# Causal attention in four head groups: blocks of two groups taken alternately, rising then falling

## The reference

```
q = einsum('bthc,oc->btho', xh, Wq) * scale
k = einsum('bthc,oc->btho', xh, Wk) * scale
v = einsum('bthc,oc->btho', xh, Wv)
scores = einsum('bihc,bjhc->bhij', q, k)
scores = where(j > i, -inf, scores)
attn = softmax(scores)
y = einsum('bhij,bjhc->bihc', attn, v)
```

## Time and profile before

| what | us |
|---|---|
| median of three runs | 2280.57 |
| lowest and highest | 2272.59, 2297.14 |
| the profiled execution | 2295.76 |
| its span, first to last instruction | 2293.9 |
| TensorE busy in the span | 2093.4 (91%) |
| VectorE busy | 1768.3 (77%) |
| ScalarE busy | 1439.4 (63%) |
| GpSimd busy | 518.1 (23%) |

### The profile page before, as it was taken

One profiled execution on the slowest core, in us unless ns is written; L12 is line 12 of the kernel. 1 busy time (PEld: TensorE's weight loads), 2 busy tenths in 40 slices (PEclk: granted clock), 3 DMA queues, 4 the chain that ended last, 5 costly groups with the idle time before them and its releaser, 6 DMA issues. The chain is left out here.

```text
span 2293.9 us, 43529 instructions
## 1 busy us (share of the span) xinstructions
PE 2093.4 (91%) x17338; PEld 1091.1 (48%) x17338; DVE 1768.3 (77%) x2212; ACT 1439.4 (63%) x2798; POOL 518.1 (23%) x772
## 2 busy tenths in 40 slices
PE   7689999999999999999999999999885959999994
PEld 5233333334444443444444433333365748787883
DVE  6476799999999878899999987776358636666666
ACT  5234577778888877678888888888732323333331
POOL 2000001100110100110111010000163646666661
PEclk9755799999999999999999999999976879999997
DMA  6815011111611111521111011000074323333336
GB/s 232 241 29 65 29 34 39 53 36 34 102 51 34 44 35 39 82 54 34 44 49 60 25 41 37 23 14 12 2 260 186 130 76 110 115 114 113 115 114 243
DMA packets 120813, 180.75 MB, mean 79 GB/s; under 512 B 15793, under 2 KB 80306, under 8 KB 119842
## 3 DMA queue, kind: packets, MB, share of 16 engines
q1 hardware_dynamic: 111904, 154.45, 23.7%
q0 software_dynamic: 6720, 19.01, 2.3%
q10 hardware_dynamic: 1986, 4.51, 0.5%
HBM read 99.92 MB, written 77.60 MB: 77 GB/s over the span
## 5 line engine op out<-in xcount | busy, mean ns | idle before, releaser
L775 DVE TENSOR_REDUCE mx<-S 128x2 f32<-128x1024 f32 (+3 forms) x1152 | 1279.7, 1134 | 206.1 <-PE S L688 131.8
L756 ACT ACTIVATE prob<-ST 128x512 f32<-128x512 f32 (+3 forms) x2304 | 1169.5, 559 | 360.0 <-PE ST L709 315.5
L723 PE MATMUL O<-prob,V 128*17 128x256 f32 (+1 forms) x8704 | 690.6, 391 | 0.3 <-POOL prob L666 0.3
L688 PE MATMUL S<-K,Q 48*128 48x512 f32 (+3 forms) x2304 | 573.9, 496 | 31.4 <-DVE mx L775 20.6
L709 PE MATMUL ST<-Q,K 49*128 49x512 f32 (+3 forms) x2304 | 493.5, 425 | 36.3 <-ACT prob L756 30.8
L688 PEld LDWEIGHTS S<-K,Q 48*128 48x128 f32 x2304 | 225.3, 192 | 472.6 <-issue 297.0
L666 POOL TENSOR_SCALAR_AFFINE_SELECT prob<-prob 128x512 f32<-128x512 f32 x128 | 81.4, 636 | 1217.6 <-ACT prob L756 1217.6
L709 PEld LDWEIGHTS ST<-Q,K 49*128 49x128 f32 x2304 | 225.3, 192 | 137.7 <-ACT prob L756 105.0
L723 PEld LDWEIGHTS O<-prob,V 128*17 128x17 f32 x8704 | 145.6, 96 | 288.9 <-issue 279.9
L1575 ACT ACTIVATE sg<-hg 128x512 f32<-128x512 f32 x92 | 55.2, 600 | 156.9 <-PE hu L1504 152.9
L1683 DVE TENSOR_TENSOR alo<-sg,ahi 128x512 fp32r<-128x512 f32 x92 | 88.1, 958 | 68.1 <-ACT ahi L1579 63.6
(11 more groups left out here) (238 smaller groups left out, 1765.4 us busy)
## 6 DMA issues: line engine op xcount, KB each, us to landing
cwb<-cwt SPq DMA_DIRECT2D x76, 256.0 KB, 4.9
lists<-wbd SPq DMA_DIRECT2D x132, 138.0 KB, 2.2
Q<-qs SPq DMA_DIRECT2D x192, 64.0 KB, 2.4
xs<-lists SPq DMA_DIRECT2D x19, 552.0 KB
K<-ks SPq DMA_DIRECT2D x18, 512.0 KB, 15.6
qs<-hl SPq DMA_DIRECT2D x16, 512.0 KB, 4.5
ks<-hl SPq DMA_DIRECT2D x16, 512.0 KB, 4.4
wraw<-in_wcat SPq DMA_DIRECT2D x54, 128.0 KB, 2.1
```

What stands on the lines that cost most here:

```text
L688: ins = pe.matmul(out[:, ab, 0:w], Q[g, n % QR, p, r * P:(r + 1) * P], K[G % 2][g, p, c * BW:c * BW + w], start=True, stop=not diag)
L723: ins = pe.matmul(O[32 * a:32 * a + VC, c0:c1], V[:, G, k, VC * a:VC * (a + 1)], prob[:, s % NP, a, c0:c1], start=s in FIRST and h == 0, s ...
L756: act.activation(prob[:, s % NP, 2 * p + ab, c0:BW], ST[u % ST_BANKS][:, c0:BW], ACT.Exp).then_inc(s_exp, 1)
L775: dve.tensor_reduce(mx[:, n % 2, a:a + step + 1:step, c], S[slot % S_RING][:, :, 0:w], AX_X, ALU.max).then_inc(s_free, 1)
```

## The change

`block_order` gives the order (0,0), (0,1), (1,0), (0,2), (1,1), (0,3), (1,2), ... (0,7), (1,6), (1,7), and then the mirror image with groups 2 and 3: (2,7), (2,6), (3,7), (2,5), (3,6), ... (2,1), (3,2), (2,0), (3,1), (3,0). Before, group 0 rose, 1 fell, 2 rose and 3 fell. The marks are now those of all blocks, from which the ones below the upper hull are dropped. K of group 1 is loaded in the three pieces like that of group 0, piece 0 at once, piece 1 at steps 0 to 2 and piece 2 at steps 8 to 10, on the semaphores of group 0's pieces; K of group 2 follows when block (0,7) has been read. Lines are 5 to 16 further down behind the places that the diff touches.

```diff
-BLOCKS = [(G, j) for G in range(NG4) for j in (range(NB) if G % 2 == 0 else range(NB - 1, -1, -1))]
+def block_order():
+    up = [(0, 0)] + [x for j in range(1, NB) for x in ((0, j), (1, j - 1))] + [(1, NB - 1)]
+    return up + [(G + 2, j) for G, j in reversed([(1 - G, j) for G, j in up])]
+
+
+BLOCKS = block_order()
...
-    marks = [(FIRST[n] - 3.0, upto[n]) for n in range(len(BLOCKS)) if n <= NB or n >= 3 * NB]
+    marks = []
+    for n in range(len(BLOCKS)):
+        x, y = FIRST[n] - 3.0, upto[n]
+        while len(marks) > 1 and (marks[-1][1] - marks[-2][1]) * (x - marks[-2][0]) <= \
+                (y - marks[-2][1]) * (marks[-1][0] - marks[-2][0]):
+            marks.pop()
+        marks.append((x, y))
...
+    events.extend(("K", (1, i, 0)) for i in range(6))
     scores(0)
...
-        if 0 <= s - 16 < 6:
-            events.append(("K", (1, s - 16, None)))
+        for i, first in ((1, 0), (2, 8)):
+            if 0 <= s - first < 3:
+                events.extend(("K", (1, 2 * (s - first) + h, i)) for h in range(2))
         for G2 in (2, 3):
-            first = LAST[NUMBER[(G2 - 2, 7 if G2 == 2 else 0)]] + 4
+            first = LAST[NUMBER[(G2 - 2, NB - 1)]] + 4
...
                         if G > 1:
-                            need("st", s_st, HG * (TPB * NB * (NB + 1) // 2) * (G - 1))
-                        load_k_part(sp, t, d, G, i // 3, i % 3, 0, T, s_k[G])
+                            need("st", s_st, units_before(NUMBER[(G - 2, NB - 1)]))
+                            load_k_part(sp, t, d, G, i // 3, i % 3, 0, T, s_k[G])
+                        else:
+                            need(f"piece{piece}", s_piece[piece], 16 * 6)
+                            load_k_part(sp, t, d, G, i // 3, i % 3, *PIECES[piece], s_piece[piece])
...
-                            if G:
+                            if G > 1:
                                 need(f"k{G}", s_k[G], 16 * 6)
-                        if G == 0:
+                        if G < 2:
                             i = 0 if c == 0 else 1 if c < 4 else 2
-                            need(f"piece{i}", s_piece[i], 16 * 6)
+                            need(f"piece{i}", s_piece[i], 16 * 6 * (G + 1))
```

More of the change, by code:

```diff
@@ L576, in attend @@
         s_piece = t["s_piece"]
-        s_k = [None] + [sem(f"k{G}_in") for G in range(1, NG4)]
+        s_k = [None, None] + [sem(f"k{G}_in") for G in range(2, NG4)]
         s_q = t["s_q"]
@@ L611, in _ @@
                     if kind == "K":
-                        G, i, _ = e
+                        G, i, piece = e
                         if G > 1:
-                            need("st", s_st, HG * (TPB * NB * (NB + 1) // 2) * (G - 1))
-                        load_k_part(sp, t, d, G, i // 3, i % 3, 0, T, s_k[G])
+                            need("st", s_st, units_before(NUMBER[(G - 2, NB - 1)]))
[3 more added lines that the diff above has]
+                            load_k_part(sp, t, d, G, i // 3, i % 3, *PIECES[piece], s_piece[piece])
                     elif kind == "Q":
```

## The result

The changed kernel took 2329.9 us (median of 20 runs, 2293.5 to 2356.5), the kernel before 2293.1 beside it on the same chip (20 runs, 2272.6 to 2326.2). The ratio is 1.0092, 95% interval 1.0054 to 1.0129: slower, by about the 1% that the prediction calls the limit of a measurement. The ratio leaves out the runs more than 1.5% above a kernel's fastest, 10 of the change's 20, and with them part of what the change adds, for over all 20 runs on each side the means are 2326.4 and 2293.8, 33 us or 1.4% apart. The profiled execution took 2319.4 us with a span of 2317.5.

A forecast was written before the change was run, and what follows sets the result against it. The prediction took 2.50 us a step at TensorE's upper clock as attention's floor. Terms 0 + 13 + 4 - 9 + 2 + 1 = +11 us gave 2306.8 for the profiled execution, 2291.6 for the median, range 2253 to 2332.

The forecast's parts named there:

- the forecast's own: Range of the main case for the whole kernel's time, 2270 to 2312 us, given a chance of 0.45.
- Pace of the maxima: Attention's half steps with two maximum jobs: as many as before, spreading them changes nothing; 0 us, bounds -10 and +2.
- The start: Opening of attention: TensorE's clock rises at about 258 us against 226, 32 us later; +13 us.
- rival 1: Opening and short blocks: the clock rises no later and falls once as before; -6 us, 2274.6, chance 0.20.
- Further falls: Short blocks reached at 2.4 GHz in the rising part: a third of a clock fall more; +4 us, -13 to +26.
- The middle: Turn between the halves: six blocks of 24 to 32 steps lose the old middle's excess; -9 us, bounds -9 and 0.
- K of group 1: Early in attention: its second piece, queued ahead of block (0,1)'s row of maxima, delays that row; +2 us, 0 to +8.
- The end: Last short blocks, under two jobs a step: 40 steps cost 0.04 us more each; +1 us, +14 if the clock falls.
- Rival 2: All of attention: spread doubles let VectorE keep up, no gap opens, the clock doesn't fall; -32 us, 2248.6, chance 0.15.
- Rival 3: Opening: the clock stays at 1.2 GHz while short blocks alternate, up to step 64; +54 us, 2334.6, chance 0.20.

The follow-up runs named there:

- fall_half: The kernel before with only groups 2 and 3 interleaved, groups 0 and 1 in their old order; ratio to before 1.0055.
- rise_half: The changed kernel with only groups 0 and 1 interleaved, group 2 rising and group 3 falling as before; ratio to before 1.0076.
- quiet_after: The changed kernel with one maximum job in each half of every block's third to tenth steps, while jobs last; ratio to before 0.9997.
- k_spread: The changed kernel with the six 512 KB loads of K of groups 2 and 3 issued every three steps, not every step; ratio to before 1.0051.
- open_warm_before: The kernel before with the matmul pair of each of the 20 maximum jobs ahead of step 0 computed twice; ratio to before 1.0013.
- tail_warm: The changed kernel with scores computed twice in the 48 half steps without a job from step 476 on; ratio to before 1.0148.

## Why the prediction came out as it did

The forecast was 2291.6, +11 us on the profiled time, with a chance of 0.54 for a change within 1%. Measured: a ratio of 1.0092, 21 us, and 33 us in the means. The sign and the likeliest class were right. The size was a half to a third of what came, the median, 2329.9, lies 2 us inside the range of 2253 to 2332 and outside the forecast's own (before's median had itself gone from 2280.6 to 2293.1 with 20 runs), and most of the reason was another: that the sum came out on the right side is in good part luck.

*Pace of the maxima (0).* The doubles are as many, as the prediction had it, and each costs little more where it stands now. 16 of them lie in steps 64 to 144, which take 215.5 us, 2.69 a step, at the upper level: (215.5 - 80 x 2.52)/16 = 0.87 us each, against the 0.76 read from the earlier trace rows, and at the prediction's upper bound of 0.86. That is 2 us for these 16. But the rest of the time rises by 10 us where the sum's terms without the clock, 0 - 9 + 2 + 1, make it fall by about 6, and none of them has this. 4.7 of it come in fall_half, whose doubles stand as before's, and 6.0 in rise_half. An even deal takes 7.5 of the 10 away, but in steps 64 to 144 only 1.3 (214.2 in quiet_after), so where the rest of the 10 lies stays open.

*The start (+13).* Wrong. The clock was up at 162, within the short blocks, down again from 189 to 227 and up from then to 650 but for 7 us at 281: the earlier trace rows had been read as a rule ("it rises in a run of wide steps") from two rises. Steps 0 to 12 took 49.3 us, predicted 55.7. The opening's time at 1.2 GHz is the same for both orders within its scatter. By the prediction's own sign, a clock up by 226, this run was rival 1's, whose time was 6 us less and not 33 more: the sign looked only at the opening.

*Further falls (+4).* This was the term that carries the result, and the one most undersized. It counted short blocks in the rising part and took a third of a fall. The falls came behind narrow steps where jobs were dealt unevenly (15 of the 17 at ninth steps), in long blocks too, and in the falling half and at the end as well. 72 us more at 1.2 GHz at 0.36 are +26 us. The price of a low microsecond, 0.37 to 0.4 in the prediction, held (0.36).

*The middle (-9).* Right in itself: blocks (1,6) and (1,7) took (931.10 - 779.62)/60 = 2.52 us a step. But the six loads of K moved with the order, the gap of 1.94 us and the low stretch came with them, and steps 228 to 432 took the same as before, +0.5. In k_spread's trace they took 1338.67 - 825.08 = 513.6 us, 8.5 less than before, as forecast.

*K of group 1 (+2).* 0. SyncE issued the row at 138.40, as worked out (139.6), but the transfers ahead of it did not hold it up: the first 512-wide scores of (0,1) started at 146.68, before at 146.45.

```profile
136.53 1.82 SPq L66 DMA_DIRECT2D K<-ks  x4
138.40 1.33 SPq L640 DMA_DIRECT2D Q<-mrow  x2
```

*The end (+1, to +14).* Steps 432 to 576 took 26 us more. At the upper level blocks (2,4) to (2,2) took (1535.62 - 1302.22)/92 = 2.54 a step against 2.50, +3; most of the rest lies in the windows from 1554 to 1586 and from 1650 to the end: 71 us at 1.2 GHz against 13, and 58 x 0.36 = 21. The bound of +14 allowed for one fall.

*The rivals.* Rival 2, that spread doubles let VectorE keep up, is refuted by the 9 us more that VectorE stood waiting and by the 2.69 a step. Rival 3, low until the short blocks end, is refuted by the rises at 162 and 227. (Rival 2's sum leaves out the + 2 + 1 that the other sums have; with them it is -29, 2251.6.) Rival 1 had the opening right and missed all the rest. The sentence that the prediction quotes from the Trainium skill, "TensorE: Matmul & The Clock Gate", What's actually happening, that activity releases the throttle, was set against the row of 130 to 226. open_warm_before shows the same again, 66 us at 1.2 GHz with TensorE busy 63.87 of them, so busy time as the profile counts it does not tell when the clock rises.

## What to carry to other kernels

Where the clock of TensorE decides, look at how the work meets at the places with less work, not at the total of it: here the same jobs dealt one to each half beside the narrow steps took back the whole loss of the new order, and made the old one 0.6% faster. A new order moves transfers too, and behind them an engine can stand though nobody waits for their data. And a pattern read from two stretches of one execution is no rule: split many runs into time at the low clock and the rest, and see how widely the first scatters, before giving it a term.

## What was not expected of the hardware

- A run's time follows its time at 1.2 GHz with 0.35 us a microsecond over 227 runs, and 2.9 us left over; the spread of 60 us between runs of one kernel is nearly all of this kind.
- TensorE stayed at 1.2 GHz while busy without a gap, as in the 11 us from 650 to 661 (11.00 busy), and ran at 0.99 of its upper level over the 40 us of tail_warm's end with 33.33 busy.
- TensorE stood 1.94 us with no semaphore behind it, some 18 us after the first of six loads of 512 KB issued within 4 us, and seven traces of seven show it; it was gone when they went out over 28 us. An instruction packet of 1.9 us ends just ahead of it in all seven, but six loads as fast for group 2 have no such gap, so what connects them is open.
